# Sharing the second butterfly stage of a ternary feed-forward between VectorE and GpSimd

## The reference, cut to what matters

```python
def act_quant(x):                       # per token, 8 bits
    scale = 128 / clip(max(abs(x), axis=-1), 1e-5)
    return clip(round(x * scale), -128, 127) / scale

def fwht(x):                            # over n = 2048, h = 1, 2, 4, ... 1024
    while h < n:
        x = x.reshape(-1, n // (2 * h), 2, h)
        a, b = x[..., 0, :], x[..., 1, :]
        x = stack([a + b, a - b], axis=-2).reshape(-1, n)
        h *= 2
    return x / sqrt(n)

gate = act_quant(x) @ ternary(w_gate).T         # 512 -> 2048
up   = act_quant(x) @ ternary(w_up).T           # 512 -> 2048
z    = silu(gate) * up
out  = act_quant(fwht(z)) @ ternary(w_down).T   # 2048 -> 512
x    = layernorm(x + out)
```

## Time and profile before

| | |
|---|---|
| median of 3 runs | 1826.65 us |
| the profiled execution, its own time | 1828.94 us |
| its span, first to last instruction | 1826.8 us |
| granted TensorE clock, mean | 0.957 |
| TensorE busy (whole span) | 1612.8 us, 88% |
| VectorE busy (whole span) | 1308.1 us, 72% |
| ScalarE busy (whole span) | 937.8 us, 51% |
| GpSimd busy (whole span) | 684.0 us, 37% |

### The profile page before, as it was taken

One profiled execution on the slowest core, in us unless ns is written; L12 is line 12 of the kernel. 1 busy time (PEld: TensorE's weight loads), 2 busy tenths in 40 slices (PEclk: granted clock), 3 DMA queues, 4 the chain that ended last, 5 costly groups with the idle time before them and its releaser, 6 DMA issues. The chain is left out here.

```text
span 1826.8 us, 26352 instructions
## 1 busy us (share of the span) xinstructions
PE 1612.8 (88%) x8780; PEld 1136.3 (62%) x8812; DVE 1308.1 (72%) x2362; ACT 937.8 (51%) x1932; POOL 684.0 (37%) x638
## 2 busy tenths in 40 slices
PE   7999978999857899997589989999889979999995
PEld 5788865555425456565466656566657757687774
DVE  6476757666768899995468486684849979876674
ACT  3221216777655556664357456364644545555552
POOL 5034344766512232322222132221322215565563
PEclk9999999999977899998899999999899999999998
DMA  6200018533020000000512112121313100000000
GB/s 207 70 24 1 9 38 227 166 97 111 3 94 1 1 1 1 1 1 0 164 39 70 53 53 70 35 70 53 100 36 118 54 29 1 1 24 1 24 23 24
DMA packets 66848, 95.71 MB, mean 52 GB/s; under 512 B 12176, under 2 KB 28688, under 8 KB 66716
## 3 DMA queue, kind: packets, MB, share of 16 engines
q1 hardware_dynamic: 58460, 80.40, 14.4%
q0 software_dynamic: 6144, 12.60, 2.6%
q10 hardware_dynamic: 2112, 1.05, 0.2%
HBM read 56.25 MB, written 4.19 MB: 33 GB/s over the span
## 5 line engine op out<-in xcount | busy, mean ns | idle before, releaser
L2659 PE MATMUL bank<-fp_xT,fp_weights_values 128*128 128x512 f32 x704 | 185.2, 402 | 14.4 <-DVE fp_gate L2559 11.6
L1520 ACT ACTIVATE causal_probs<-bank,causal_neg 128x512 f32<-128x512 f32 (+3 forms) x256 | 134.3, 531 | 114.2 <-DVE causal_neg L1612 74.3
L2659 PEld LDWEIGHTS bank<-fp_xT,fp_weights_values 128*128 128x128 f32 x704 | 129.6, 189 | 58.1 <-DVE fp_gate L2559 19.0
L2684 PE MATMUL bank<-fp_wd,fp_hT 128*128 128x512 f32 x528 | 133.2, 393 | 4.7 <-DVE X L2581 3.5
L1410 POOL DMA_DIRECT2D causal_qS<-causal_qk x96 | 48.2, 508 | 228.2 <-DVE causal_qk L1570 227.8
L2568 DVE SCALAR_TENSOR_TENSOR fp_up<-bank,fp_weights_scales,fp_up 128x512 f32<-128x512 f32 x132 | 99.1, 751 | 44.0 <-ACT fp_up L2465 36.5
L779 ACT ACTIVATE heads_probs<-bank,heads_neg 128x512 f32<-128x512 f32 x128 | 88.2, 690 | 79.0 <-DVE heads_neg L815 79.0
L815 DVE TENSOR_REDUCE heads_neg<-bank 128x1 f32<-128x512 f32 x128 | 86.8, 680 | 56.5 <-PE bank L860 56.3
L964 POOL TENSOR_TENSOR ternary_z<-ternary_z 128x1024 f32<-128x1024 f32 x16 | 37.7, 2354 | 217.6 <-DVE ternary_z L1111 217.6
L2684 PEld LDWEIGHTS bank<-fp_wd,fp_hT 128*128 128x128 f32 x528 | 98.5, 188 | 28.5 <-issue 6.7
L1207 PE MATMUL bank<-weights_raw,ternary_qT 128*128 128x512 bf16 x433 | 105.8, 390 | 7.9 <-ACT weights_raw L618 5.7
(11 more groups left out here) (256 smaller groups left out, 4150.1 us busy)
## 6 DMA issues: line engine op xcount, KB each, us to landing
pairs_xd<-X SPq DMA_DIRECT2D x64, 128.0 KB, 2.7
pairs_cd<-in_ctx SPq DMA_DIRECT2D x64, 128.0 KB, 2.8
causal_qS<-causal_qk SPq DMA_DIRECT2D x96, 64.0 KB, 2.8
causal_qS<-causal_qk POOLq DMA_DIRECT2D x96, 64.0 KB, 2.5
causal_kS<-causal_qk SPq DMA_DIRECT2D x96, 64.0 KB, 2.6
causal_kS<-causal_qk POOLq DMA_DIRECT2D x96, 64.0 KB, 2.5
X<-in_x SPq DMA_DIRECT2D x4, 1024.0 KB, 7.7
heads_cT<-in_ctxT SPq DMA_DIRECT2D x4, 1024.0 KB, 6.1
```

What stands on the lines that cost most here:

```text
L1520: act.activation(probs_of(i)[:, h + one], view[:, one], ACT.Exp, bias=neg[:, G % 2, at:at + 1], accum_out=total[:, G % 2, at:at + 1]).then ...
L2659: last = pe.matmul(banks[4 + g][:], values[:, g, n % NI, of], xT[:, part, g], start=part == 0, stop=part == 1)
L2684: last = pe.matmul(banks[t][:], hT[:, n % SLOTS, a, t * P:(t + 1) * P], wd[:, c, i], start=i == 0 and k == 0, stop=i == NI - 1 and k == 2)
```

## The change

GpSimd gets a third instruction per tile: the differences of stage 0 (h = 256), behind its own first butterfly. VectorE keeps the sums of stage 0. A new semaphore `half_done` counts the differences, and VectorE waits for it before stages 1 and 2 of the same tile. Nothing else is changed: the arithmetic is the same, and so are the buffers.

```diff
+        half_done = m.sem("half_done")
...
                     butterflies(pool, z[:, t % 2], z1[:, t % 2], 1).then_inc(first_done, 1)
+                    pool.wait_ge(first_done, t + 1)
+                    if t >= 2:
+                        pool.wait_ge(z_turned, CH * (t - 1))
+                    s, d = halves(z1[:, t % 2], 2), halves(z2[:, t % 2], 2)
+                    pool.tensor_tensor(d[:, :, 1], s[:, :, 0], s[:, :, 1], ALU.subtract).then_inc(half_done, 1)
                 if t == 3:
                     past.clear(pool, norm.var_ready)
                 norm.root(pool, 0, t - 3)
...
                     dve.wait_ge(first_done, t + 1)
                     if t >= 2:
                         dve.wait_ge(z_turned, CH * (t - 1))
-                else:
-                    dve.wait_ge(butterfly, 3 * t + n)
+                    s, d = halves(src[:, t % 2], 2), halves(dst[:, t % 2], 2)
+                    dve.tensor_tensor(d[:, :, 0], s[:, :, 0], s[:, :, 1], ALU.add).then_inc(butterfly, 1)
+                    return
+                dve.wait_ge(butterfly, 3 * t + n)
+                dve.wait_ge(half_done, t + 1)
                 butterflies(dve, src[:, t % 2], dst[:, t % 2], 2 << n).then_inc(butterfly, 1)
```

## The result

The changed kernel takes 1847.58 us (median of 4 runs, 1845.84 to 1851.03) against 1826.6 us before. The ratio is 1.0118, 95% interval 1.01 to 1.0135: slower by 21 us. The forecast was 1843.5 us, range 1836 to 1850. The median lies above the 1840 to 1847 that the forecast's own case allowed, and inside the whole range. The profiled execution took 1848.93 us (span 1847.1), 20.0 us more than that of before; the forecast's sum was +16.9.

A forecast was written before the change was run, and what follows sets the result against it. VectorE was taken to set the ternary step, with the chain through GpSimd's root equally long. A 2.76 us delay less 1.13 saved gives +1.63 a step, +16.9 in all: 1843.5 us, range 1836 to 1850.

The forecast's parts named there:

- the forecast's own case: Ternary stage: VectorE's rounding gets the ports first, GpSimd's operation is held; +1.63 us a step, +16.9 in all; 70%.
- The short chain: Ternary step: fourth z chunk, two GpSimd additions, root, L206; no slack, so L206 comes 2.76 us later.
- The new operation: GpSimd's third operation, ahead of the root: 2.36 us like its siblings, starting 0.17 us after the first butterfly.
- the margin to L1188: VectorE's rounding of y was to start 0.10 us ahead of GpSimd's new operation and so get the ports.
- GpSimd first: Rival, 12%: GpSimd takes the shared ports before VectorE's rounding; +1.66 us a step, +20.9 us in all.
- Step 3: Ternary stage, third step: existing waits swallow the saving and the new operation ends before the root is needed; 0 us.
- The tail: End of the ternary stage, L206 of step 15: delay of 1.63 us less 1.09 us of existing wait; +0.54 us.
- the first rival: GpSimd takes the shared ports first, drawing out VectorE's rounding; 19.94 us a step, 1847.5 us in all; 12%.
- the root's row: Earlier profile: the root's record began 0.06 us before VectorE's rounding, yet the root was drawn out, 1.32 us for 0.55.
- a cap: TensorE's chain limits a ternary step to 17.95 us, 0.33 us below VectorE's 18.28, whatever VectorE saves.
- a chain hanging from L1188: TensorE's work from the rounding's end to the fourth gate and up matmuls, 10.88 us, plus 0.09 to the next chunk.
- Steps 1, 2, 4 and 14: Ternary stage edges: +0.56 us each in 1 and 2 from held GpSimd, saving alone in 4, +0.06 for 14's L206.

The follow-up runs named there:

- VectorE always first: Changed kernel plus a wait on GpSimd, so its new operation starts only after VectorE's rounding L1188 has ended; 1849.93 us, ratio 1.0119.
- the saving alone: Kernel before, with stage 0's differences left out on VectorE for tiles 2 to 15 and nothing added on GpSimd; 1819.61 us, ratio 0.9962.
- the kernel with GpSimd first: Changed kernel plus a wait on VectorE, so its rounding L1188 starts only after GpSimd's new operation; 1855.56 us, ratio 1.0152.

## Why the prediction held, and where it was off

- *The bound.* Right. The short chain from the fourth z chunk over GpSimd to L206 had no slack. With nothing else changed, an operation put into it comes out as an idle time of 2.75 us before L206 (forecast 2.76).
- *The new operation.* Right: 2.34 to 2.36 us where the ports are free (forecast 2.36). Its start was off: GpSimd's wait for itself cost 0.08 us here, not the 0.17 us of the earlier trace rows, so the margin to L1188 was 0.00 to 0.02 us and not 0.10. This is the one mis-sized term that mattered. In the steps where VectorE is first it changes nothing, because the hold ends with L1188; the step came out at 19.83 us for a forecast of 19.91.
- *Who is first.* I gave "GpSimd first" 12% as a case of the whole kernel. It turned out to be a matter of single steps: 4 of 14 in one execution, 3 in the other. In the steady part of the main run such a step adds 0.8 us (step 6, where the clock fell as well) or 0.15 us (step 7). Step 3, which I put at zero, cost 2.0 us: L1188 of step 2 was drawn out, and TensorE began the transposes behind it 2.2 us later than before. The tail with step 15's rounding cost 2.1 us where I said 0.54, for the same reason. These two are 3.6 us above the forecast, and the rest of the sum is 0.2 us below it, which makes +20.3 of +16.9. The experiment with VectorE always first bears out 2.7 of the 3.6: it gives 0.6 us for the tail, my figure, but step 3 still costs 0.85 us there.
- *The number.* The 1847.58 us are within 0.1 us of the first rival's 1847.5, and that is chance: most steps are of the forecast's kind. The forecast's own case, +16.9 us, was 3 to 4 us short of the measured 20 to 21.
- *The lock rule.* The Trainium skill's page "SBUF — State Buffer", section "Who interferes with whom", says that whoever issues first gets the shared pair of ports for the whole instruction, and that the other is blocked. The traces agree on the hold: the loser waits out the winner's whole instruction (3.42 us for 1.23, or 3.43 for 2.36). On who wins they show only the recorded starts, and these decide to within some 0.01 us: GpSimd won with 0.01 us of lead in step 6 and lost with the same lead in step 11. What the root's row had suggested, that GpSimd can lose with a recorded start ahead, holds for a long operation too, though the lead lost is 0.01 us and not 0.06.
- *TensorE.* Right as a cap (17.79 us with the saving alone, forecast 17.95) and as a chain hanging from L1188 (10.96 us for a forecast of 10.97). Its gap before these transposes, forecast at 1.96 us, was 1.69 us in the changed kernel and left the clock at 1.00; the gap of 3.88 us in step 6 did not (the stretch from 660 to 680 has 0.91).
- *Steps 1, 2, 4 and 14.* +1.2 (steps 1 and 2), -1.1 and 0.0 us for forecasts of +1.1, -1.1 and +0.06. The step behind L206 of step 14 has the 17.78 us that it had before. Stage 1 of tile 0 did wait for the new operation, held behind VectorE's sums (idle time 1.65 us).

Three things stay open. The 0.85 us that step 3 costs even with VectorE first were not traced to one cause (in that trace the sums of stage 0 are held 3.03 us beside the waiting operation, and the clock in that stretch is 0.57). The third of a microsecond that step 3's root came later than the rest of its step has no explanation. And how far the executions differ in the number of GpSimd-first steps was seen in two traces only; the spread of the times doesn't show it.

## What to carry to other kernels

An engine with 12 us of idle time in a step of 18 can still stand on the critical path: look at what is queued behind the place where work is to go, and who waits for that within the same step. Then look at what the other engine does beside it; here a long operation of each did not overlap when both wanted the shared ports, and the second ended more than 1 us late. The same 2.36 us of GpSimd work cost 21 us in front of a root that VectorE waits for, 11 us behind that root, and gained 7 us in an empty stretch next to a z chunk and a reduce.

## What the runs showed of the hardware that I had not expected

- A held instruction is cheaper than a waiting one: GpSimd's operation ended 2.20 us behind L1188 when it had begun and was held, and 2.52 us behind it when a semaphore released it.
- A VectorE tensor_scalar on 128x2 values was held by GpSimd (0.91 us for 0.21), while its neighbours on 128x1 values, just before it and within the same 2.36 us of GpSimd, were not (0.15 and 0.16 us). Small size does not protect an instruction.
- TensorE's clock after an idle gap, by the time of the 16 transposes behind it (1.07 us full, 1.89 us fallen): full after 1.69 and 2.03 us, full in one step and fallen in another after 2.27 us, fallen after 3.88 us in the changed kernel, and yet full after 3.42 us in the kernel with GpSimd first. The length of the gap alone does not tell.
- The recorded starts of two operations that compete for the ports tell which one won only if they are more than 0.01 us apart for long operations; the root (128x1) lost with 0.06 us of lead.
- GpSimd's wait for its own semaphore cost 0.17 us in the rope stage and 0.08 us here.
